# A mixture-of-experts block: the tokens' weights become rows through DRAM instead of on TensorE

## What is computed

```python
x = x + 0.5 * ffn(layernorm(x)); x = x + attention(layernorm(x)); x = x + 0.5 * ffn(layernorm(x))

def ffn(x):                                    # E = 8 experts, K = 2, D = O = 256
    probs = softmax(x @ gate_w + gate_b, axis=tokens)
    vals, idx = top_k(probs, 2)
    h = relu(x @ w1[e] + b1[e]); h = relu(h @ w2[e] + b2[e]); y = relu(h @ w3[e] + b3[e])
    w_tok[token, e] = vals where e is chosen, else 0
    v[e] = sum over tokens of y[e, token] * w_tok[token, e]
    out[token] = sum over the chosen e of v[e]
```

## Time and profile before

| what | value |
|---|---|
| median of 3 runs | 2264.23 us (2263.72 to 2271.89) |
| the profiled execution's own time | 2265.92 us |
| its span, first to last instruction | 2264.2 us |
| mean granted TensorE clock | 0.973 of full speed |
| first expert stage, tiles | from 82 to 318 us |
| second expert stage, tiles | from 2005 to 2242 us |

### The profile page before, as it was taken

How to read it: one execution, slowest core, us unless ns; L and a number is a source line. 1 busy time by engine, 2 the same in 40 slices (tenths; PEclk the granted TensorE clock), 3 DMA queues, 4 the chain that set the end, 5 groups by cost and what they waited for, 6 DMA issues and landing times.

```text
span 2264.2 us, 98001 instructions
## 1 busy us (share of the span) xinstructions
PE 2152.1 (95%) x42449; PEld 1871.4 (83%) x42449; DVE 1855.9 (82%) x3881; ACT 1612.2 (71%) x3536; POOL 533.9 (24%) x1311
## 2 busy tenths in 40 slices
PE   4799989999999999999999999999999999789997
PEld 2688866389999999999999899998999997568885
DVE  6655556699999999999999999999999993765555
ACT  2344445488888888888888888888888887334442
POOL 2333302421221221312212212122122211033330
PEclk9799989999999999999999999999999999879998
DMA  6411102410010100101101001010010002141112
GB/s 205 120 44 49 47 8 91 154 38 11 25 29 7 32 23 13 32 7 29 27 9 32 16 20 32 4 32 25 11 32 11 25 4 86 30 120 46 47 47 81
DMA packets 95527, 96.23 MB, mean 43 GB/s; under 512 B 41332, under 2 KB 84088, under 8 KB 95096
## 3 DMA queue, kind: packets, MB, share of 16 engines
q0 software_dynamic: 42048, 44.80, 7.9%
q1 hardware_dynamic: 52624, 45.15, 6.3%
q10 hardware_dynamic: 424, 0.01, 0.0%
HBM read 64.14 MB, written 25.43 MB: 40 GB/s over the span
## 4 chain that ended last, share of the span: by engine, by line
PE 89%; DVE 4%; issue 3%; ACT 1%; POOL 1%; DMA 1%; SPq 1%; ACTq 0%; POOLq 0%; DVEq 0%
PE bank L1090 43%; PE bank L1082 19%; PE bank L991 18%; PE bank L1128 2%; PE bank L1002 1%; PE bank L1045 1%; PE bank L1193 1%; PE bank L971 1%; DVE rows L1241 1%; DVE stats L1223 1%; PE bank L1009 1%; PE bank L1136 1%; PE bank L1058 0%; SPq L624 0%; DVE x_res L1492 0%
## 5 line engine op out<-in xcount | busy, mean ns | idle before, releaser
L1090 PE MATMUL bank<-work 96*32 96x512 bf16 (+4 forms) x17920 | 1411.9, 362 | 2.8 <-DVE work L1531 2.3
L830 ACT ACTIVATE feat<-bank 128x512 f32<-128x512 f32 (+3 forms) x2304 | 1251.3, 565 | 152.2 <-PE bank L1090 75.3
L1531 DVE TENSOR_REDUCE work<-bank 128x1 f32<-128x512 f32 (+3 forms) x2176 | 1298.4, 639 | 62.1 <-PE bank L1090 50.3
L1082 PE MATMUL bank<-feat,phase 128*17 128x128 f32 x16896 | 1138.1, 272 | 2.4 <-issue 2.4
L1082 PEld LDWEIGHTS bank<-feat,phase 128*17 128x17 f32 x16896 | 829.5, 98 | 67.8 <-issue 3.1
L1090 PEld LDWEIGHTS bank<-work 96*32 96x32 bf16 (+1 forms) x17920 | 807.3, 96 | 68.0 <-DVE work L1531 11.1
L991 PE MATMUL bank<-work 128*128 128x256 f32 x1872 | 435.1, 382 | 3.6 <-issue 2.0
L991 PEld LDWEIGHTS bank<-work 128*128 128x128 f32 x1872 | 340.7, 191 | 53.9 <-issue 12.3
L1429 DVE COPY work<-phase 128x514 f32 x234 | 100.5, 430 | 190.6 <-ACT work L779 60.7
L563 POOL TENSOR_SCALAR_AFFINE_SELECT feat<-feat 128x128 f32<-128x128 f32 x512 | 146.6, 294 | 442.5 <-ACT feat L830 435.9
L505 POOL DMA_INDIRECT work<-token_table,row_no x156 | 149.8, 961 | 327.7 <-DVE work L1443 243.6
(11 more groups left out here) (173 smaller groups left out, 1417.1 us busy)
## 6 DMA issues: line engine op xcount, KB each, us to landing
phase<-in_w SPq DMA_DIRECT2D x12, 1024.0 KB, 12.3
work<-qk_parts POOLq DMA_DIRECT2D x60, 192.0 KB, 4.2
token_table<-rows SPq DMA_DIRECT2D x8, 1056.0 KB, 9.6
qk_parts<-phase SPq DMA_DIRECT2D x20, 384.0 KB, 2.7
work<-qk_parts POOLq DMA_DIRECT2D x60, 128.0 KB, 4.3
qk_parts<-work SPq DMA_DIRECT2D x12, 384.0 KB, 2.6
x_res<-in_x SPq DMA_DIRECT2D x8, 512.0 KB, 6.5
work<-work SPq DMA_DIRECT2D x256, 1.0 KB
```

Source lines behind the costliest of these rows:

```text
L830: eng.activation(p_ring[:, n % P_RING, lo:QB], s_bank("probs", n)[:, lo:QB], ACT.Exp, scale=HD ** -0.5).then_inc(sig.s_done, 1)
L1082: mm = eng.matmul(bank[ACC_BANK][GRID * g:GRID * g + VW, 0:P], v_aug[:, t, h, :], p_ring[:, n % P_RING, g * P:(g + 1) * P], start=(t == 0) ...
L1090: mm = eng.matmul(out[GRID * g:GRID * (g + 1), width], left[:, GRID * g:GRID * (g + 1)], right, start=start, stop=stop)
L1531: eng.tensor_reduce(maxima[:, h % 2, j, i, k + 1:k + 2], scores[:, 0:hi - lo], AX_X, ALU.max).then_inc(sig.a_done, 1)
```

## The change

SyncE gets a new sequence of 39 pairs of transfers per expert stage, `weight_rows`, right after `store_table`. For each tile it waits for VectorE's reduce (two signals per tile now, not three), stores the 256 weights, 2 neighbouring values from each of 128 partitions, to DRAM, waits until they have landed, and loads them back broadcast to all 128 partitions into the ring of 4 rows. The row holds the weights in the order (partition, half); the layers' results have the order (half, partition), so weighing reads the row with a step of 2 values.

TensorE's two weight transpositions, VectorE's copy 128 wide and ScalarE's copy of the row are taken out. The reduce into `w_col` now waits for the store of two tiles before. Weighing waits for the load. x's transpositions go to bank 0 and bank 1 in turn, and wait for the copy of the tile two before instead of one before.

```diff
@@ -188,6 +188,11 @@
         yield "divide", u
 
 
+def w_row_uses(f, j):
+
+    return f * len(range(j % 2, N_TILES, 2)) + j // 2 + 1
+
+
 class Waits:
 
 
@@ -231,7 +236,7 @@
 
         self.slot = [many(f"slot_loaded{f}_", NXG) for f in range(2)]
         self.staged, self.xt, self.xt_copy = many("staged", 2), many("tile_tr", 2), many("tile_copied", 2)
-        self.w_col, self.w_tr, self.w_row = many("weight_col", 2), many("weight_tr", 2), many("weight_row", 2)
+        self.w_col, self.w_stored, self.w_row = many("weight_col", 2), one("weight_stored"), many("weight_row", 2)
         self.layer = [many(f"layer_mm{f}_", LAYERS) for f in range(2)]
         self.relu_a, self.relu_v = many("relu_by_scalar", 2), many("relu_by_vector", 2)
         self.weighted, self.v_part = many("weighted", 2), many("v_partial", 2)
@@ -281,6 +286,7 @@
         gate_b_sb = sb("gate_b_sb", [P, E])
         bank = [ctx.enter_context(nc.psum_tensor(f"bank{i}", [P, QB], F32)) for i in range(8)]
         table = [nc.dram_tensor(f"token_table{f}", (S + 1, ROW), F32).ap() for f in range(2)]
+        w_dram = nc.dram_tensor("tile_weights", (2, N_TILES, TILE), F32).ap()
         parts_dram = nc.dram_tensor("qk_parts", (2, 3, D, S), BF16).ap()
 
 
@@ -348,7 +354,6 @@
         acts = carve(3 * 2 * KD * TILE).rearrange("p (l b k s) -> p l b k s", l=3, b=2, k=KD)
         weighted = carve(2 * KD * TILE).rearrange("p (b m s) -> p b m s", b=2, m=KD)
         w_row = carve(W_RING * TILE).rearrange("p (b s) -> p b s", b=W_RING)
-        w_wide = carve(2 * TS * P).rearrange("p (b u s) -> p b u s", b=2, u=TS)
         w_pick = carve(2 * TS * E).rearrange("p (b u e) -> p b u e", b=2, u=TS)
         w_col = carve(2 * TS).rearrange("p (b u) -> p b u", b=2)
         chosen_wide = work[:, WORK - NT * V_ROWS // 2:WORK].bitcast(BF16).rearrange("p (i c) -> p i c", i=NT)
@@ -499,7 +504,7 @@
                 need.wait_ge(sig.zero, 32)
                 need.wait_ge(sig.table[f], 16 * GROUPS)
                 need.wait_ge(sig.xt[f], 4 * (j - NXG + 1))
-                need.wait_ge(sig.w_col[f], 3 * (j - NXG + 1))
+                need.wait_ge(sig.w_col[f], 2 * (j - NXG + 1))
                 for u in range(TS):
                     n = j * TS + u
                     eng.indirect_dma_start(
@@ -598,6 +603,16 @@
                     eng.dma_start(table[f][1:S + 1, :].rearrange("(i p) r -> p i r", p=P)[:, g * GRP:(g + 1) * GRP, :],
                                   rows[:, g * GRP:(g + 1) * GRP, :]).then_inc(sig.table[f], 16)
 
+            def weight_rows(f):
+
+                for j in range(N_TILES):
+                    need.wait_ge(sig.w_col[f], 2 * (j + 1))
+                    eng.dma_start(w_dram[f, j].rearrange("(p u) -> p u", u=TS), w_col[:, j % 2]).then_inc(sig.w_stored, 16)
+                    need.wait_ge(sig.w_stored, 16 * (f * N_TILES + j + 1))
+                    need.wait_ge(sig.w_row[j % 2], 16 * (w_row_uses(f, j) - 1))
+                    need.wait_ge(sig.weighted[f], KD * (j - W_RING + 1))
+                    eng.dma_start(w_row[:, j % W_RING], w_dram[f, j].partition_broadcast(P)).then_inc(sig.w_row[j % 2], 16)
+
             def store_parts(n):
                 ob, sc = CHUNKS[n]
                 b, qk, r0 = n % SPLIT_BF, ob // KD, (ob % KD) * P
@@ -635,6 +650,7 @@
             eng.dma_start(w_qkv_sb[:, :, :], w_qkv_t.rearrange("(k p) o -> p k o", p=P)).then_inc(sig.attw, 16)
             eng.dma_start(w_out_sb[:, :, :], w_out_t.rearrange("(k p) o -> p k o", p=P)).then_inc(sig.attw, 16)
             store_table(0)
+            weight_rows(0)
             for n in range(EARLY_CHUNKS):
                 store_parts(n)
                 if n % 2 == 0 and n >= 4:
@@ -658,6 +674,7 @@
                             "o (i p) -> o i p", p=P), max_rows[m * TPJ:(m + 1) * TPJ, b, :]).then_inc(sig.max_row[b], 16)
             load_experts(1)
             store_table(1)
+            weight_rows(1)
             for g in range(GROUPS):
                 need.wait_ge(sig.x_added[1], (g + 1) * GRP // 2)
                 eng.dma_start(out_rows[:, g * GRP:(g + 1) * GRP, :],
@@ -766,11 +783,8 @@
                     if j < N_TILES:
                         need.wait_ge(sig.xt[f], 4 * (j + 1))
                         need.wait_ge(sig.layer[f][0], j - 1)
-                        eng.activation(acts[:, 0, j % 2].rearrange("p k s -> p (k s)"), bank[0][:, :],
+                        eng.activation(acts[:, 0, j % 2].rearrange("p k s -> p (k s)"), bank[j % 2][:, :],
                                        ACT.Copy).then_inc(sig.xt_copy[f], 1)
-                        need.wait_ge(sig.w_tr[f], TS * (j + 1))
-                        need.wait_ge(sig.weighted[f], KD * (j - W_RING + 1))
-                        eng.activation(w_row[:, j % W_RING], bank[1][:, 0:TILE], ACT.Copy).then_inc(sig.w_row[f], 1)
                     j = n - 1
                     if 0 <= j < N_TILES:
                         need.wait_ge(sig.layer[f][0], j + 1)
@@ -885,7 +899,6 @@
                         need.wait_ge(sig.feat[n], m - 1)
                         if n == 1:
                             need.wait_ge(sig.xt_copy[0], N_TILES)
-                            need.wait_ge(sig.w_row[0], N_TILES)
                         if n == 2:
                             need.wait_ge(sig.s_done, S_ALL)
                         for i in range(i0, i0 + 4):
@@ -995,19 +1008,12 @@
 
             def transpose_tile(f, j):
                 need.wait_ge(sig.slot[f][j % NXG], 32 * (j // NXG + 1))
-                need.wait_ge(sig.xt_copy[f], j)
+                need.wait_ge(sig.xt_copy[f], j - 1)
                 need.wait_ge(sig.chosen_copy[f], NT // 4)
                 for u in range(TS):
                     for k in range(KD):
-                        eng.transpose(bank[0][:, k * TILE + u * P:k * TILE + (u + 1) * P],
+                        eng.transpose(bank[j % 2][:, k * TILE + u * P:k * TILE + (u + 1) * P],
                                       x_slot[:, j % NXG, u, k * P:(k + 1) * P], ident[:, :]).then_inc(sig.xt[f], 1)
-
-            def transpose_weight(f, j):
-                need.wait_ge(sig.w_col[f], 3 * (j + 1))
-                need.wait_ge(sig.w_row[f], j)
-                for u in range(TS):
-                    eng.transpose(bank[1][:, u * P:(u + 1) * P], w_wide[:, j % 2, u],
-                                  ident[:, :]).then_inc(sig.w_tr[f], 1)
 
             def tiles(f):
                 for j in range(N_TILES + LAYERS):
@@ -1015,8 +1021,6 @@
                     if j < N_TILES:
                         transpose_tile(f, j)
                     layer(f, j - 2, 1)
-                    if j < N_TILES:
-                        transpose_weight(f, j)
                     layer(f, j - 1, 0)
                 need.wait_ge(sig.v_part[f], KD * N_TILES)
                 need.wait_ge(sig.routed[f], ROUTED["position"])
@@ -1430,26 +1434,26 @@
                                 experts[:, bass.ds(expert, 1), l, :].rearrange("p a w -> p (a w)"),
                                 ).then_inc(sig.staged[f], 1)
 
-            def widen_weight(f, j):
+            def pick_weight(f, j):
                 b = j % 2
                 need.wait_ge(sig.slot[f][j % NXG], 32 * (j // NXG + 1))
                 need.wait_ge(sig.routed[f], ROUTED["tile_mask"])
                 eng.tensor_tensor(w_pick[:, b], x_slot[:, j % NXG, :, D:ROW],
                                   bc(tile_mask[:, j, :], 1, [P, TS, E]), ALU.mult).then_inc(sig.w_col[f], 1)
-                need.wait_ge(sig.w_col[f], 3 * j + 1)
+                need.wait_ge(sig.w_col[f], 2 * j + 1)
+                need.wait_ge(sig.w_stored, 16 * (f * N_TILES + j - 1))
                 eng.tensor_reduce(w_col[:, b], w_pick[:, b], AX_X, ALU.add).then_inc(sig.w_col[f], 1)
-                need.wait_ge(sig.w_col[f], 3 * j + 2)
-                need.wait_ge(sig.w_tr[f], TS * (j - 1))
-                eng.tensor_copy(w_wide[:, b], bc(w_col[:, b], 2, [P, TS, P])).then_inc(sig.w_col[f], 1)
 
             def weigh(f, j):
                 need.wait_ge(sig.layer[f][2], j + 1)
-                need.wait_ge(sig.w_row[f], j + 1)
+                need.wait_ge(sig.w_row[j % 2], 16 * w_row_uses(f, j))
                 need.wait_ge(sig.v_part[f], KD * (j - 1))
+                by_tile = w_row[:, j % W_RING].rearrange("p (s u) -> p u s", u=TS)
                 for m in range(KD):
                     eng.scalar_tensor_tensor(
-                        weighted[:, j % 2, m], bank[4][:, m * TILE:(m + 1) * TILE],
-                        staged[:, j % 2, 2, KD * D + m:KD * D + m + 1], w_row[:, j % W_RING], ALU.add, ALU.mult,
+                        weighted[:, j % 2, m].rearrange("p (u s) -> p u s", u=TS),
+                        bank[4][:, m * TILE:(m + 1) * TILE].rearrange("p (u s) -> p u s", u=TS),
+                        staged[:, j % 2, 2, KD * D + m:KD * D + m + 1], by_tile, ALU.add, ALU.mult,
                     ).then_inc(sig.weighted[f], 1)
 
             def relu_second(f, j):
```

(2 more changed lines are left out.)

## The result

The changed kernel takes 2304.6 us (median of 4 runs, 2298.11 to 2311.48) against 2263.97 us before: a ratio of 1.0173, 95% interval [1.0159, 1.0187]. It is slower by 1.7%, where I forecast 2248 us and faster. The profiled execution is its quickest, 2298.1 us with a span of 2296.4, 32 us above that of before.

A forecast was written before the change was run, and what follows sets the result against it. In the expert stages TensorE's work and VectorE's ordered round were taken to bind at nearly one pace. TensorE's 17 us off 2265.9 gives 2248.9, by the median 2247.2; VectorE may hold back a microsecond: 2248 us, range 2243 to 2262.

The forecast's parts named there:

- TensorE's part of the sum, 17 us: Expert stages: dropping two weight transpositions per tile, 0.22 us of each tile's chain, saves TensorE 17 us if VectorE keeps up.
- VectorE keeps up with 0.20 to 0.25 us less: VectorE's round per tile: without the widening copy it shrinks 0.20 to 0.25 us, against TensorE's 0.22, nothing to spare.
- my fourth rival: VectorE's round shrinks less than TensorE's work (new waits cost 0.1 us or weighing starts no sooner): 2252 to 2255; chance 0.08.
- The stepped read, nothing: VectorE's weighing: reading the row with a step of two values (8 bytes) adds no time.
- both rivals that rested on it: Weighing's stepped read costs 0.38 us a tile, 2265 us, chance 0.12; or 0.53 at half rate, 2280 us, chance 0.07.
- Bank and ScalarE, nothing: x's doubled bank on TensorE and ScalarE's dropped copy (0.37 us a tile) were each forecast to gain nothing.
- Its own loop (issue, landing of the store, issue) is 3.7 to 5.7 us per tile against a period of 5.65, which it just keeps at the worse end: SyncE's transfers per tile: 0.57 us per issue and 2.6 to 4.6 us landing were taken to fit the tile period.
- The rival's mechanism: Third rival, late transfers: SyncE's loop over 5.65 us a tile or a pair over 17 us; 2300 at 6.2 us; chance 0.03.
- the two new semaphore waits (store of two tiles ago, row landed), which have long been met: VectorE's waits around reduce and weighing: claimed to take at most 0.05 us off its 0.25 us gain per tile.
- a late pair on SyncE: SyncE's queue: behind a late store and load would stand only the next pair and, after the last, the attention parts' stores.
- The DMA engines are 18% busy there: Expert stage: 128 KB more written per tile beside the gathers' 264 KB was taken as harmless, gathers running ahead.

The follow-up runs named there:

- the best version: Changed kernel with two stores in flight, four places for picked weights, each stage's first store held until the second tile's pick: 2249.4 us, repeated 2248.5 us.

## Why the prediction was wrong

- **TensorE's part of the sum, 17 us: right.** The run with no transfers gains 14 us, the three with the store's pieces apart 16.5 to 17.9 (one run each, 2247.3 to 2247.9 against 2263.8 to 2265.6), the best version 17.
- **VectorE keeps up with 0.20 to 0.25 us less: right.** Tiles came every 5.62 us wherever nothing waited for a transfer. As long as the transfers are in time, the waits by which my fourth rival would have come about cost nothing that shows: weighing follows the reduce within 0.1 us.
- **The stepped read, nothing: right** (477 ns against 476), and with it both rivals that rested on it fell.
- **Bank and ScalarE, nothing: right**, the bank by a run of its own.
- **The step that failed: "Its own loop (issue, landing of the store, issue) is 3.7 to 5.7 us per tile against a period of 5.65, which it just keeps at the worse end".** The landing was bounded by a store of long pieces and a small load, and neither writes short pieces side by side to DRAM. Store to load was 6.07 us, not 2.6 to 4.6 plus an issue. Worse, the upper end, 5.7 us, already passed the period of 5.65, and I still gave the case 0.03. A bound that touches the limit, for a shape that no row shows, deserved a chance like that of the stepped read. The rival's mechanism ("SyncE's loop would have to take over 5.65 us a tile for many tiles") was the one that came true. Its size has a slip: with 78 us for every microsecond beyond 5.65, on top of 2247, a loop of 6.2 us gives 2290 and not 2300. The same sum with the measured 6.4 us gives 2306, near the 2304.6 measured.
- **With it failed "the two new semaphore waits (store of two tiles ago, row landed), which have long been met".** I named what stood behind a late pair on SyncE, but not that VectorE's reduce waits for the store with a ring of only two, so that a late store stops weighing, the ReLUs and TensorE at once: 33.2 us of VectorE's waits in one stage. The run with a ring of four shows this to be about two thirds of the loss.
- **"The DMA engines are 18% busy there": a share was read as room.** A 1 KB store per tile raised it to nearly half, with hardly any bytes of its own: the gathers' packets, as many as before, took more than twice their time.

## What to carry to other kernels

Cost a small transfer by its pieces and where they land, not by its bytes: 128 pieces of 8 bytes side by side in DRAM landed in 4.2 us and slowed all that ran beside them, the same pieces 32 or more bytes apart did not. Where an engine issues a transfer, waits for its landing and issues the next, its loop time is a bound like that of any busy engine: write it beside the period, and if the two are close, put two in flight and give the ring that feeds it more places. A forecast whose worse end only just fits should carry the chance that it doesn't.

## What was not expected of the hardware

- Neighbouring 8-byte writes to DRAM hold up the DMA engines, and the time shows in the records of the other queue: the gathers' queue took 44.6% of the engines against 18.7% with the same bytes, and a gather landed in 4.7 us instead of 2.8. At 32, 64 and 512 bytes apart: 18.3, 18.7 and 18.2% (one run each). Where the limit lies between 8 and 32 bytes, and what in the memory makes it, is open.
- In one partition of SBUF the same neighbouring pieces landed in 1.9 us without harm; but a load that reads one partition's kilobyte 128 times took SyncE's queue, loads and stores, to 39.3% of the engines, where the loads from DRAM took 9.0%.
- Store and load, each harmless alone (2249.7 and 2251.5 us), cost 53 us together.
